# A recurrent net, a mixture of experts and attention in one kernel: eight weight buffers in the prologue, and expert tiles with fewer products

## The reference

```
def _L0_cond_ref(...):                  # GRU, 256 steps one after another, state 8 x 512
    def cell(h, x):
        gi = x @ W_ih + b_ih
        gh = h @ W_hh + b_hh
        r, z = sigmoid(i_r + h_r), sigmoid(i_z + h_z)
        n = tanh(i_n + r * h_n)
        h_new = (1.0 - z) * n + z * h
    _, hs = jax.lax.scan(cell, initial_state, xs)

def _L0_ffn_ref(...):                   # 8 experts of width 192, the best 2 for each token
    scores = einsum('bsd,ed->bse', x, w_gate_router)
    topk_scores, topk_idx = jax.lax.top_k(scores, 2)
    weights = softmax(topk_scores) spread over the experts
    gate = einsum('bsd,efd->bsef', x, w_gate_proj)
    up = einsum('bsd,efd->bsef', x, w_up_proj)
    out = einsum('bsef,edf,bse->bsd', silu(gate) * up, w_down_proj, weights)

x = x + _L0_ffn_ref(_L0_cond_ref(cond_2048, x, ...), ...)
x = x + _L1_ffn_ref(_L1_cond_ref(x, cond_2048[:, None, :], ...), ...)
# L1: adaptive norm and attention of 16 heads, then a gated ternary feed-forward net of width 1408
```

## Time and profile before

| | |
|---|---|
| median of 3 runs | 1795.61 us (1793.72 to 1798.26) |
| the profiled execution | 1789.96 us |
| its span, first to last instruction | 1788.2 us |
| granted TensorE clock, mean | 0.901 |
| PE busy | 1593.9 us (89%), 32043 products |
| DVE, ACT, POOL busy | 1184.0 (66%), 911.5 (51%), 601.9 us (34%) |
| DMA | 90.76 MB, mean 51 GB/s |

### The profile page before, as it was taken

The page is one execution under the profiler, slowest core; times in us unless marked ns, Lnnn a source line. Parts: engine busy times, 40 slices in busy tenths (PEclk is TensorE's granted clock), DMA queues, the critical chain, the costliest instruction groups (busy, mean ns, idle before and its releaser), DMA issues. The chain is left out here.

```text
span 1788.2 us, 76589 instructions
## 1 busy us (share of the span) xinstructions
PE 1593.9 (89%) x32043; PEld 1222.2 (68%) x32043; DVE 1184.0 (66%) x4252; ACT 911.5 (51%) x3320; POOL 601.9 (34%) x1805
## 2 busy tenths in 40 slices
PE   6999999999999999997399974788888887799999
PEld 5999999999999999997266642355555555544444
DVE  5778888887877778887744427565666676573231
ACT  5555555555555556555245445366666677432130
POOL 0333333333333333333445434143333333580000
PEclk9999999999999999655599985798989889799999
DMA  5110101111100111101447444000000000130001
GB/s 173 45 31 11 50 20 41 29 29 40 49 25 5 34 45 46 37 22 57 150 130 252 132 145 145 35 1 1 2 2 1 2 1 2 42 100 23 26 0 48
DMA packets 45735, 90.76 MB, mean 51 GB/s; under 512 B 6736, under 2 KB 25296, under 8 KB 45392
## 3 DMA queue, kind: packets, MB, share of 16 engines
q1 hardware_dynamic: 38992, 64.89, 11.6%
q0 software_dynamic: 6400, 20.98, 3.5%
HBM read 66.90 MB, written 18.87 MB: 48 GB/s over the span
## 5 line engine op out<-in xcount | busy, mean ns | idle before, releaser
L402 PE MATMUL bank<-arena 128*128 128x8 f16 x12288 | 501.2, 170 | 9.7 <-issue 5.1
L405 PE MATMUL bank<-arena 128*128 128x16 f16 x12288 | 496.8, 182 | 3.1 <-issue 2.2
L402 PEld LDWEIGHTS bank<-arena 128*128 128x128 f16 x12288 | 412.0, 97 | 39.1 <-ACT bank L498 19.1
L405 PEld LDWEIGHTS bank<-arena 128*128 128x128 f16 x12288 | 412.3, 97 | 4.3 <-issue 3.2
L664 POOL TENSOR_TENSOR arena<-arena 128x16 f32<-128x16 f32 x512 | 116.8, 228 | 542.7 <-DVE arena L607 527.9
L468 ACT ACTIVATE arena<-arena 128x16 f32<-128x16 f32 x512 | 114.6, 224 | 307.0 <-DVE arena L586 306.7
L597 DVE TENSOR_TENSOR_SCAN arena<-arena,bank 128x64 f32<-128x64 f32 x512 | 147.1, 287 | 19.4 <-ACT arena L468 2.5
L586 DVE TENSOR_REDUCE arena<-bank 128x16 f32<-128x48 f32 x512 | 100.2, 196 | 84.4 <-PE bank L405 79.3
L1958 PE MATMUL bank<-arena 128*128 128x512 f16 x704 | 152.3, 379 | 1.7 <-PEq L1461 1.7
L375 PE MATMUL bank<-arena 128*128 128x256 f16 x1008 | 148.6, 274 | 1.6 <-issue 1.6
L1496 PE MATMUL bank<-arena 128*128 128x512 f16 x576 | 142.7, 402 | 4.5 <-DVE arena L1752 4.5
(11 more groups left out here) (202 smaller groups left out, 2752.5 us busy)
## 6 DMA issues: line engine op xcount, KB each, us to landing
arena<-yrows SPq DMA_DIRECT2D x16, 512.0 KB, 4.2
arena<-in_wgu SPq DMA_DIRECT2D x48, 128.0 KB, 2.2
arena<-in_xT SPq DMA_DIRECT2D x32, 128.0 KB, 2.2
hrows<-arena SPq DMA_DIRECT2D x16, 256.0 KB, 4.0
arena<-in_xtok SPq DMA_DIRECT2D x16, 256.0 KB, 8.9
out_y<-arena SPq DMA_DIRECT2D x16, 256.0 KB, 2.0
arena<-in_wih SPq DMA_DIRECT2D x4, 768.0 KB, 6.4
arena<-in_whh SPq DMA_DIRECT2D x4, 768.0 KB, 5.4
```

What stands on the lines that cost most here:

```text
L402: mm = nc.tensor.matmul(dst[:, j * B:(j + 1) * B, 1], w, h[:, 0], start=home not in opened, stop=False, skip_group_check=True)
L405: mm = nc.tensor.matmul(dst[:, j * B:(j + 1) * B, 1:3], w, h.rearrange("p a c -> p c a"), start=home not in opened, stop=False, skip_group ...
```

## The change

Prologue: the eight weight blocks have a buffer each (`raw_wih` where the four stood, `raw_whh` in space that is free then). `load_weight` waits for nothing. x of the first and of the second 32 steps is one transfer each. The four `wih` blocks are issued right behind x, ahead of the six small transfers; ACT and DVE split all four before their small work. In `project_x` the last row block's three products go tile by tile, so the tiles are finished one after the other. Steps 0 to 30 follow a table `FIRST_FILLS` of their own, with five products in step 0.

Expert tiles: the 192 hidden columns are laid out as three blocks of 128: high 0 to 127; high 128 to 191 beside low 128 to 191; low 0 to 127. They need three transposes, and with the last 64 rows of the down weights twice in `wdns` (now 128 partitions) five products. `turn_x` and `take_x` run two tiles ahead, not one. 39 tiles are enough for 4096 rows and 8 experts. The core of the diff:

```
-FH = F // 2
-TILES = 2 * NTOK // P + E
+FR = F - P
+TILES = (2 * NTOK + E * (P - 1)) // P
...
-                return FH, wdn[:, 2 * n * D:2 * (n + 1) * D]
+                return P, wdn[:, 2 * n * D:2 * (n + 1) * D]
...
+        raw_whh = Mem(arena, base).take([KT, G3], F32)
...
-        raw = m.take([4, G3], F32)
+        raw_wih = m.take([KT, G3], F32)
...
+        FIRST_FILLS = (0,) + (5, 5, 5, 5, 4) * 5 + (4,) * 6
         FILLS = (5, 5, 5, 5, 4, 5, 5, 5, 5, 4, 4, 4, 4, 4, 4, 4) * 2
...
-            return window + 1, range(sum(FILLS[:i]) if t > 0 else 0, sum(FILLS[:i + 1]))
+            fills_at = FILLS if window > 0 else FIRST_FILLS
+            return window + 1, range(sum(fills_at[:i]), sum(fills_at[:i + 1]))
...
                 def load_weight(i):
-                    if i >= 4:
-
-                        sp.wait_ge(w_lo, i - 3)
                     src = wih if i < KT else whh
-                    sp.dma_start(raw[:, i % 4, :], src[:, i % KT, :]).then_inc(raw_in[i % 4], 16)
+                    sp.dma_start(raw(i), src[:, i % KT, :]).then_inc(raw_in[i], 16)
...
-                load_x(0, 0)
-                load_weight(0)
+                sp.dma_start(xc[:, :, half_of(0)], xT[:, :, bass.ts(0, GC)]).then_inc(x_in[0], 16)
+                for i in range(KT):
+                    load_weight(i)
                 sp.dma_start(cst[:, :], consts).then_inc(small_in, 16)
...
-                for i in range(1, 2 * KT):
+                for i in range(KT, 2 * KT):
                     load_weight(i)
-                load_x(1, 0)
+                sp.dma_start(xc[:, :, half_of(1)], xT[:, :, bass.ts(1, GC)]).then_inc(x_in[1], 16)
...
-                    for k in range(KT):
+                    for k in range(KT - 1):
...
+                    k = KT - 1
+                    pe.wait_ge(x_lo, KT)
+                    pe.wait_ge(w_lo, KT)
+                    for mt in range(n_first):
+                        b, half = FIRST_SLOTS[mt]
+                        for n, (wp, xp) in enumerate(((0, 0), (0, 1), (1, 0))):
+                            mm = nc.tensor.matmul(bank[b][:, half_of(half)], wihs[:, wp, k, mt, :], xs[:, xp, k, half_of(0)],
+                                                  start=False, stop=(n == 2), skip_group_check=True)
+                        mm.then_inc(gi_mm, 1)
...
-                high_w(0)
+                for i in range(KT):
+                    high_w(i)
                 act.wait_ge(small_in, 6 * 16)
...
-                low_w(0)
+                for i in range(KT):
+                    low_w(i)
                 dve.wait_ge(small_in, 6 * 16)
...
-        wdns = m.take([2, 2, E, D], F16, FH)
+        wdns = m.take([2, 2, E, D], F16)
...
-                    for part in range(2):
-                        for half in range(2):
-                            at = (2 * part + half) * P
-                            mm = nc.tensor.transpose(bank[4 + i % 2].bitcast(F16)[0:FH, at:at + P],
-                                                     hid[:, i % 2, part, half * FH:(half + 1) * FH], id1[:, :])
+                    for at in range(0, 3 * P, P):
+                        mm = nc.tensor.transpose(bank[4 + i % 2].bitcast(F16)[:, at:at + P], hid[:, i % 2, at:at + P],
+                                                 id1[:, :])
...
-                    for h_, w_ in ((0, 0), (0, 1), (1, 0)):
-                        for half in range(2):
-                            mm = nc.tensor.matmul(bank[6 + i % 2][:, :], hidT[0:FH, i % 2, h_, half, :],
-                                                  wdns[0:FH, w_, half, bass.ds(e, 1), :], start=(n == 0), stop=(n == 5))
-                            n += 1
+                    for slot, w_, rest in ((0, 0, 0), (0, 1, 0), (1, 0, 1), (1, 1, 1), (2, 0, 0)):
+                        mm = nc.tensor.matmul(bank[6 + i % 2][:, :], hidT[:, i % 2, slot, :],
+                                              wdns[:, w_, rest, bass.ds(e, 1), :], start=(n == 0), stop=(n == 4))
+                        n += 1
...
-                    if 0 < i < TILES - 1:
-                        turn_x(i + 1)
+                    if i < TILES - 2:
+                        turn_x(i + 2)
...
-                    V.tensor_tensor(hid[:, i % 2, 1, :], hf[:, i % 2, :], hid[:, i % 2, 0, :],
+                    V.tensor_tensor(hid[:, i % 2, F:2 * P], hf[:, i % 2, P:F], hid[:, i % 2, P:F], ALU.subtract)
+                    V.tensor_tensor(hid[:, i % 2, 2 * P:3 * P], hf[:, i % 2, 0:P], hid[:, i % 2, 0:P],
                                     ALU.subtract).then_inc(hid_lo, 1)
...
-                    if 0 < i < TILES - 1:
-                        take_x(i + 1)
+                    if i < TILES - 2:
+                        take_x(i + 2)
```

More of the change, by code:

```diff
@@ L169, in raw_count @@
         def raw_count(n):
-            return 16 * sum(PARTS if i < NGU else 1 for i in range(n % 3, n + 1, 3))
+            return 16 + 16 * sum(PARTS if i < NGU else 1 for i in range(n % 3, n + 1, 3))
         def load_raw_part(sp, n):
@@ L221, in mixed_net_kernel @@
         ABS_AT = {first + i: (c, i) for c, first in enumerate((34, 66, 98, 130)) for i in range(3 * ABS)}
+        FIRST_FILLS = (0,) + (5, 5, 5, 5, 4) * 5 + (4,) * 6
         FILLS = (5, 5, 5, 5, 4, 5, 5, 5, 5, 4, 4, 4, 4, 4, 4, 4) * 2
-        assert len(FILLS) == TG and sum(FILLS) == 12 * GM
+        assert len(FILLS) == len(FIRST_FILLS) == TG and sum(FILLS) == sum(FIRST_FILLS) == 12 * GM
         def filled(t):
@@ L244, in mixed_net_kernel, with raw @@
         HALF = [slice(0, 16), slice(16, 32)]
+        def raw(i):
+            return raw_wih[:, i, :] if i < KT else raw_whh[:, i - KT, :]
         small_in = sem("small_in")
-        raw_in = [sem(f"raw_in{i}") for i in range(4)]
         x_in = two("x_in")
+        we_in = sem("we_in")
+        raw_in = [sem(f"raw_in{i}") for i in range(KT)] + raw3_in + [we_in]
         wal_in = sem("wal_in")
@@ L259, in mixed_net_kernel @@
         pads = sem("pads")
-        we_in, ss_mm, ss_done = sem("we_in"), sem("ss_mm"), sem("ss_done")
+        ss_mm, ss_done = sem("ss_mm"), sem("ss_done")
         gi_staged, gi_tail = sem("gi_staged"), sem("gi_tail")
@@ L350, in project_x @@
                             b, half = FIRST_SLOTS[mt]
-                            mm = nc.tensor.matmul(bank[b][:, half_of(half)], wihs[:, 1, k, mt, :], xs[:, 0, k, half_of(0)],
-                                                  start=False, stop=(k == KT - 1), skip_group_check=True)
-                            if k == KT - 1:
-                                mm.then_inc(gi_mm, 1)
+                            nc.tensor.matmul(bank[b][:, half_of(half)], wihs[:, 1, k, mt, :], xs[:, 0, k, half_of(0)],
+                                             start=False, stop=False, skip_group_check=True)
+                    k = KT - 1
[7 more added lines that the diff above has]
+                        mm.then_inc(gi_mm, 1)
                     for mt in range(n_first, GM):
@@ L416, in shift_part @@
                     if n == 0:
-                        pe.wait_ge(we_in, 16 * 4 * KT)
+                        pe.wait_ge(we_in, 16 + 16 * 4 * KT)
                         pe.wait_ge(gi_evac, NGC * GM)
@@ L438, in high_x @@
                 def high_x(c, k):
-                    act.wait_ge(x_in[c % 2], 16 * KT * (c // 2 + 1))
+                    act.wait_ge(x_in[c % 2], 16 + 16 * KT * (c // 2))
                     A.activation(xs[:, 0, k, half_of(c)], xc[:, k, half_of(c)], ACT.Copy, scale=SX).then_inc(x_hi, 1)
                 def high_w(i):
-                    act.wait_ge(raw_in[i % 4], 16 * (i // 4 + 1))
+                    act.wait_ge(raw_in[i], 16)
                     w = wihs if i < KT else whhs
-                    A.activation(w[:, 0, i % KT].rearrange("p a b -> p (a b)"), raw[:, i % 4, :], ACT.Copy,
+                    A.activation(w[:, 0, i % KT].rearrange("p a b -> p (a b)"), raw(i), ACT.Copy,
                                  scale=SW).then_inc(w_hi, 1)
@@ L573, in _ @@
                                     None, ALU.mult)
+                V.memset(ones16[:, :], 1.0).then_inc(consts_done, 1)
                 dve.wait_ge(h_init, 4)
                 V.tensor_tensor(mv[:, 1, 1, :, 2], inh[:, :, 2], mv[:, 1, 0, :, 2], ALU.subtract).then_inc(h_init, 1)
-                for i in range(1, 2 * KT):
+                for i in range(KT, 2 * KT):
                     low_w(i)
@@ L735, in mixed_net_kernel @@
         hf = m.take([2, F], F32)
-        hid = m.take([2, 2, F], F16)
-        hidT = m.take([2, 2, 2, P], F16, FH)
+        hid = m.take([2, 3 * P], F16)
+        hidT = m.take([2, 3, P], F16)
         yo = m.take([3, D], F32)
@@ L1001, in high_hidden @@
                         act.wait_ge(th_mm, i - 1)
-                    A.activation(hid[:, i % 2, 0, :], hf[:, i % 2, :], ACT.Copy).then_inc(hid_hi, 1)
+                    A.activation(hid[:, i % 2, 0:F], hf[:, i % 2, :], ACT.Copy).then_inc(hid_hi, 1)
                 def take_hidden(i):
@@ L1007, in take_hidden @@
```

(7 more changed lines are left out.)

11 lines of the change are left out of this document (4 added, 7 removed).

## The result

The changed kernel takes 1773.66 us (median of 4 runs, 1768.56 to 1778.96), the kernel before on the same chip 1795.3 us (4 runs, 1793.72 to 1798.26): 21.6 us less, a ratio of 0.9878 with a 95% interval of 0.9846 to 0.991. The forecast was 1773.5. The profiled execution took 1772.59 us with a span of 1770.8, at a mean granted clock of 0.902.

A forecast was written before the change was run, and what follows sets the result against it. Prologue bound by weight-block transfers pacing ACT, expert tiles by the ring through `gate_up` and `take_x`, PE's work 0.1 us below. Gains 6.1 - 0.7 + 16.7 = 22.1 us, so 1795.6 - 22.1 = 1773.5; range 1768 to 1781.

The forecast's parts named there:

- case A: Whole kernel: the forecast itself holds, 1773.5 us, own range 1769 to 1778; chance 0.57.
- Prologue, forecast 5.3 for the first step: Prologue: weight blocks no longer wait for buffers, so the GRU's first step starts at 29.6 us, not 34.87.
- Case C: Prologue gives little: first block later or 24 products at low clock; 2.6 in place of 6.1, 1777 us; chance 0.15.
- gains nothing by itself: Prologue: splitting the last row block tile by tile is worth nothing, as ACT arrives about when PE is done.
- Step 0 and the fills, forecast 0.8 net: First GRU steps: five fewer products in step 0 save 1.1 us, five later steps pay 0.3; bounds 0 and 1.1.
- the stated bound of 6.4: Prologue and first steps together: upper bound of their gain, forecast 6.1 us less, bounds 2.6 and 6.4.
- Routing, forecast 0.7 lost: Routing: larger down pieces loaded between the `hrows` writes may delay them, nothing to 1.6 us; 0.7 lost taken.
- Tiles, forecast 16.7: Expert tiles: period 3.66 us in place of 4.032, 16.7 us less in all, bounds 11.5 and 18.1.
- the split of the 17.4: Expert tiles: gain of 4.0 missing tile, 8.0 sixth product, 2.0 fourth transpose, 3.4 wait; 14.2 if the wait stayed.
- The late gather, forecast 1.2 lost: Expert tiles: a gather has 6.9 us, the slowest lands in 8.1; 1.2 us lost, bounds 0 and 3.
- Case B: Expert tiles: late gathers or a wait that stays in the loop, about 1777 us, both 1780; chance 0.19.
- Case E: GRU steps: slower overall, one mechanism being a clock that stays at half after step 0; chance 0.03.

The follow-up runs named there:

- the changed kernel once more: The changed kernel with no edit, run again on another chip: 1770.66 us, ratio 0.9881 to the kernel before.
- the old products: The changed kernel with the last row block's projection products in the old order, all high ones and then all low ones: 1775.86 us.
- the old pieces: The changed kernel with the old four turned blocks, six down products and down pieces of 96 x 1024, still two tiles ahead: 1779.72 us.
- the prologue alone: The kernel before with only the edits of the prologue and the fills, the expert tiles as they were: 1786.84 us, ratio 0.9969.
- tiles alone: The kernel before with only the expert tiles changed (39 tiles, three blocks, five products, two tiles ahead): 1782.05 us, ratio 0.994.
- forty tiles: The changed kernel with 40 expert tiles in place of 39: 1772.51 us.
- one tile ahead: The changed kernel with `turn_x` and `take_x` back in their old places, one tile ahead: 1787.51 us.
- order only: The changed kernel with four raw buffers, `whh` going through those of `wih` behind a wait for their low parts: 1773.14 us.

## Why the prediction was right, and where it was not

**The sum.** Right by the median: 21.6 us less, forecast 22.1, case A. By the two profiles the span fell by 17.4 and 22.2. Between these two the GRU steps differ by 8 us, of which the other stages give 3.2 back; of this scatter the prediction knew nothing. It moved the median by its sum and gave 3 us for scatter. That the median came within 0.2 us of 1773.5 is luck: the four runs spread over 10.4 us, and the interval of the ratio is that of a gain of 16 to 28 us. On the second chip the gain was 20.9.

**Prologue, forecast 5.3 for the first step: 5.73 measured.** The first block came at 6.91 (forecast 7.4), the eighth 14.32 us behind it (14.1), the first reading at 24.09 (24.6), the 24 products took 2.79 (2.6), the step started at 29.14 (29.6). Case C, the low clock in the 24 products, did not come: they followed an idle time of 1.31 us at full speed. Of the 5.73 us, 1.69 are the first block, 2.17 the pace of the blocks and 1.87 what follows the eighth. One step came out in only some profiles, "since the idle time ahead of them shrinks from 2.7 to some 0.3 us": here PE was done with its ten tiles at 23.65, not 25.1, because it began 0.5 us earlier and only the first twenty products ran slowly, and it waited 1.31; in the changed kernel once more, where the clock rose later, it waited 0.28. It cost nothing, as ACT's readings are the later leg. That the split "gains nothing by itself" is confirmed by the old products. What the prediction left out is that buffers and order overlap.

**Step 0 and the fills, forecast 0.8 net:** 1.1 for step 0 itself, 1.05 measured at the same low clock. In the first profile step 0 lost 1.65, since the clock stayed full, so first step and step 0 together gave 7.4 us, above the stated bound of 6.4. The term that was left out is the clock of the products that stay in step 0. What the five later steps pay is below the scatter of the steps.

**Routing, forecast 0.7 lost:** 1.25 and 1.43 us more in the profiles of the change, but 0.89 with the old pieces, 0.45 in the prologue alone, and 0.38 in tiles alone, which has the larger pieces. The ten profiles with the larger pieces lie between 64.5 and 65.7 us, 65.1 in the mean, the four with the old ones between 63.9 and 65.0, 64.4 in the mean. That is the 0.7 of the forecast, but most profiles with the larger pieces have the new prologue too, and the two with it and the old pieces lie 0.8 above the two with neither. So the loss can't be put down to the pieces alone, and the forecast mechanism isn't shown: ACT still waited 12.0 us for the writes of `hrows`, where the earlier trace rows has 12.4.

**Tiles, forecast 16.7: 16.34 and 15.85 measured.** The period of 3.66 was right (3.64), and so were the missing tile (3.84 by forty tiles) and PE as the next bound. The step that failed, without harm to the total, is the split of the 17.4: "8.0 the sixth product (37 x 0.216), 2.0 the fourth transpose, 3.4 the wait. If the wait stayed, the loop would be 3.75 and the gain 14.2." The prediction had itself written that the loop was closed by the ring `gate_up`, sigmoid, `hidden`, `take_x`, and then treated its wait as a constant to be added to PE's work. A ring's period doesn't shrink with work that isn't in it: one tile ahead shows 4.03, so product and transpose alone buy nothing of the period; opening the ring alone buys 0.10 of each iteration (3.92), and only behind that do they buy 0.28. The total came out right because the change did both.

**The late gather, forecast 1.2 lost:** 1.95 in the first profile of the change (5.59 against 3.64), and 1.6 to 2.6 in the three others with that order in POOL's list and no stop of ACT. The term was mis-sized in the time that the gather has. The prediction gave it 6.9 us, with a scatter of 1.04 us ahead of it; the scatter of 947.56 took 1.92, and 6.0 were left. The 1.04 was read from an ordinary scatter; the slow one in four was in the same trace, at 1.58. The gather's landing, 7.9 us, was within the 8.1 of the earlier trace rows. Case B as a whole (1777) didn't come in the medians of the change, but tiles alone, with a gather 3.25 us late and half the clock behind it, had part of it. The Trainium skill ("DMA: Bandwidth & Descriptors", "Queues, rings and completion order") has a DMA engine take turns between queues, packet by packet. The traces agree as far as they go: the gathers are late where the token loads fill the DMA engines (tiles alone, share 1.04 and 403 GB/s), and a start of 9.5 us in place of 6.0 removes the wait. The turns themselves no run shows.

**Case E**, a clock that stays low behind step 0, did not come: the steps took 784.95 and 792.90 us with the change, and 789.86 before.

## What to carry to other kernels

When a loop is closed by a ring through several engines, write down which instructions are in the ring before pricing a saving: work outside it is worth nothing until the ring is opened, and opening the ring is worth only the distance to the next bound, so the two have to be priced together. A loop made faster takes its time from every transfer that was started a fixed number of iterations ahead; look at what stands in front of its issue in the queue, and put the transfer that someone waits for ahead of the one that nobody waits for. A change with two parts that relieve the same stretch (here buffers and issue order) should be priced by each alone, since most of the gain may come with either.

## What the runs showed of the hardware

- The 256 recurrent steps took 784.95 and 792.90 us in two executions of the same kernel; 46 and 62 single steps took over 3.2 us, 27 of them the same steps in both. Over all fourteen profiles the stage took 783.03 to 796.22 us. A difference below some 8 us in it can't be read from one profile.
- The granted clock doesn't follow the idle time ahead of a stretch alone: behind 2.70 us (before, the 24 products) and 3.25 us (tiles alone) it was 0.50; behind 1.31 and 1.49 us it was full; and behind 3.09 us in order only the next `gate_up` took 2.12 us, full speed. In the first steps it fell to 0.50 in some executions and not in others of the same code; it fell in the eight in which it had risen later in the prologue.
- Every fourth issue of a scatter on POOL is long in the first part of the tile stage, in every profile: 1.57 to 1.59 us four times in the four with the old layout of the hidden rows, 1.80 to 2.53 in the ten with the new one, where the others took 0.99. It goes to the gather behind it. No run shows why.
- ACT stood still for 2.0 to 3.6 us at a time, up to five times, in three of the profiles with the new tiles, and in none of the others. The trace names no releaser on the core.
